# A transformer layer on one core: the causal mask of the row maxima moved from TensorE to VectorE

## The chip, the core and the metric

The kernel runs on one core of a Trainium2 chip, in one launch. The core has TensorE (matrix products into PSUM), VectorE, ScalarE and GpSimd (elementwise work, reductions, masks), and queues that issue DMAs. Each engine runs its own instruction stream in order; they wait for one another through semaphores. The metric is the device time of one execution in microseconds, and the time of the kernel before is the median of three runs.

## The reference, cut to what matters

Four sublayers, each on the layer norm of a residual stream of 16 x 256 tokens with 128 channels: attention a, a mixture of experts, attention b, the same experts again. Both attentions have 16 heads and a causal mask. Attention a, cut (b has no latent space and no rotary tables, and a query and key of 8 channels a head):

```python
q_lat = q @ q2l_w.T + q2l_b                       # 32 latent channels a head; k_lat, v_lat likewise
q_lat = q_lat * cos + _rotate_half(q_lat) * sin   # k_lat likewise
q_for_k = q_lat @ wqk_w.T + wqk_b
att = jnp.einsum('bhql,bhkl->bhqk', q_for_k, k_lat) * L ** (-0.5)
att = jnp.where(causal[None, None], att, -jnp.inf)
att = jax.nn.softmax(att, axis=-1)
y_lat = jnp.einsum('bhqk,bhkl->bhql', att, v_lat)
...
return y @ cproj_w.T + cproj_b
```

## The kernel before, in words

**Stages.** Attention a, experts, attention b, experts run one after the other, each written out once per engine as that engine's instruction stream. An attention handles the 4096 tokens in 8 chunks of 512 (two sequences of 256), and each chunk in 8 units: one sequence and one group of four heads. So there are 64 units an attention.

**A unit.** For each of its four heads, TensorE makes *straight* scores, queries on partitions and keys along the row, in PSUM banks 0 to 3, one bank a head. Only three blocks of 128x128 are made, since the fourth lies above the diagonal: columns 0 to 127 hold the first 128 queries against the first 128 keys, columns 128 to 383 the second 128 queries against all 256 keys. The straight scores serve one purpose: the maximum of every row. VectorE takes it with the sign turned, into M (`row_max` in b, L858 and L859, over four heads at once; `pair_max` in a, L866 and L867, over two heads at once). TensorE turns M (`turn_max`, L1440), and the turned maxima are added to the *turned* scores, keys on partitions, in banks 4 and 5, two heads (a *pair*) at a time. ScalarE takes the exponential of a pair (`exponent`, L1176) into PT, GpSimd sets what lies above the diagonal to zero in PT (`mask`, L548), and TensorE multiplies PT with the values (`weighted`, L1451), one unit later.

**The mask, twice.** For the exponentials GpSimd's zeroes are enough. For the maxima the mask comes from TensorE: `causal` (L1433) opens each bank's accumulation with a matmul of an identity with a block of 0 and -1e30, written to the two diagonal blocks of the bank; the straight scores are added on top.

**How the maxima reach the turned scores.** In a, ScalarE copies the turned maxima (`copy_max`, L1215), and two more matmuls add them (L1499, L1501). In b, VectorE adds them to the query (`join_max`, L933), and the turned scores are made with that sum (L1575, L1579).

**Order.** The order of the work is written out by hand. In a, TensorE's unit is: turn_max, causal of banks 2 and 3, perhaps a projection (`second`), phase 0 (turned scores of heads 0 and 1 of this unit beside straight scores of heads 2 and 3 of the next), another projection, causal of banks 0 and 1, phase 1 (the other heads), a closing step, the value product of the unit before. In b it is: turn_max, causal of banks 2 and 3, a projection (`early`), a wait for join_max, causal of banks 0 and 1, all straight scores of the next unit, turned scores of pair 0, the value product of the unit before, another step (`late`), turned scores of pair 1. On VectorE the maxima stand between the closing work of the projections and the closing steps: the swap of rotary halves (L888, L890) and the low parts of queries (L896) in a; the query's closing (L830), the experts' rows (L1135) and join_max in b; layer norm statistics (L712 to L721) in both. GpSimd does the masks and, in a, the rotary tables' products (L568, L578) and the keys' low parts (L584), in b the keys' sums (L616) and gathers (L649).

**Semaphores around the change.** s_ready (TensorE: straight scores are there) is waited for by the maxima; max_ready (VectorE) by turn_max; mt_ready by copy_max or join_max; exp_done by the masks and by the turned scores that reuse the banks; masked by the value product.

Of the kernel before, what the change touches and what calls it, by code (L numbers as in the profile page):

```python
# [17 lines left out]
P = 128  # L18
# [4 lines left out]
G = 4  # L23
# [287 lines left out]
def program(nc, x, c_attn_w, c_attn_b, q2l_w, q2l_b, kv2l_w, kv2l_b, l2o_w, l2o_b, wqk_w, wqk_b, cproj_w, cproj_b,  # L311
# [7 lines left out]
    with ExitStack() as ctx:  # L319
# [15 lines left out]
        ident_b = sb("ident_b", [P, P], BF16)  # L335
        causal_b = sb("causal_b", [P, P], BF16)
# [35 lines left out]
        with ExitStack() as att:  # L372
# [3 lines left out]
            PT = sb("PT", [P, 2, G, 3 * P], F32, att)  # L376
# [155 lines left out]
        def _(pool):  # L532
# [172 lines left out]
        def _(dve):  # L705
# [73 lines left out]
            for dst, src in ((ident_b, "ident"), (causal_b, "causal"), (before_b, "before"), (sel_r, "sel")):  # L779
                own.did(v.tensor_copy(dst[:, :], con(src)))  # L780
# [73 lines left out]

            def row_max(m, unit, first):

                dve.wait_ge(m["s_ready"], unit + 1)
                v.tensor_reduce(M[:, 0, first::L], PS[:, 0:4, 0:P], AX, ALU.max, negate=True)  # L858
                v.tensor_reduce(M[:, 1, first::L], PS[:, 0:4, P:3 * P], AX, ALU.max, negate=True).then_inc(m["max_ready"], 1)  # L859

            def pair_max(m, unit, pair):
# [3 lines left out]
                banks, cols = slice(2 - 2 * pair, 4 - 2 * pair), slice((2 - 2 * pair) * L, (4 - 2 * pair) * L, L)  # L865
                v.tensor_reduce(M[:, 0, cols], PS[:, banks, 0:P], AX, ALU.max, negate=True)  # L866
                ins = v.tensor_reduce(M[:, 1, cols], PS[:, banks, P:3 * P], AX, ALU.max, negate=True)  # L867
# [282 lines left out]
        def _(act):  # L1150
# [194 lines left out]
        def _(pe):  # L1345
# [83 lines left out]
            def causal(banks):  # L1429

                for j in banks:
                    diagonal = bank[j].rearrange("p (a k) -> p a k", k=P)[:, 0:3:2, :]
                    t_.matmul(diagonal, ident_b[:, :], causal_b[:, :].unsqueeze(1).broadcast_to([P, 2, P]), start=True, stop=False,  # L1433
                              skip_group_check=True)

# [7 lines left out]
            def weighted(m, unit, g, b_, at):  # L1443
# [12 lines left out]
            def attention_a():  # L1456
# [11 lines left out]
                def phase(unit, pair, next_unit):  # L1468
# [12 lines left out]
                    for term, (q, k, kt, qt) in enumerate(((q_h, k_h, k_h, q_h), (q_l, k_h, k_l, q_h), (q_h, k_l, k_h, q_l))):  # L1481
                        if ni is not None:
                            for j, at in straight:
                                t_.matmul(bank[at][:, P:3 * P], q[rows[j], ni % 3, nb, P:S], k[rows[j], ni % 3, nb, :], start=False, stop=False, skip_group_check=True)  # L1484
                        if unit >= 0:
                            for j, at in turned:
                                t_.matmul(bank[at][:, 0:S], kt[rows[j], i3, b_, 0:P], qt[rows[j], i3, b_, :], start=(term == 0), stop=False, skip_group_check=True)
# [5 lines left out]
                        if unit >= 0:  # L1493
                            for j, at in turned:
                                t_.matmul(bank[at][:, S:S + P], kt[rows[j], i3, b_, P:S], qt[rows[j], i3, b_, P:S], start=False, stop=False, skip_group_check=True)
                    if unit >= 0:
                        pe.wait_ge(m["mt_copied"], unit + 1)
                        for j, at in turned:
                            t_.matmul(bank[at][:, 0:S], sel_r[rows[j], :], max_t[rows[j], :, :].rearrange("p b q -> p (b q)"), start=False, stop=False, skip_group_check=True)  # L1499
                        for j, at in turned:  # L1500
                            ins = t_.matmul(bank[at][:, S:S + P], sel_r[rows[j], :], max_t[rows[j], 1, :], start=False, stop=True, skip_group_check=True)  # L1501
# [14 lines left out]
                causal(range(4))  # L1516
# [3 lines left out]
                for unit in range(end):  # L1520
                    turn_max(m, unit)
                    if unit + 1 < end:
                        causal((2, 3))
# [5 lines left out]
                    if unit + 1 < end:  # L1529
                        causal((0, 1))  # L1530
# [12 lines left out]
            def attention_b():  # L1543
# [7 lines left out]
                def scores(unit):  # L1551
# [14 lines left out]
                def turned_scores(unit, pair):  # L1566
# [22 lines left out]
                causal(range(4))  # L1589
# [7 lines left out]
                for unit in range(end):  # L1597
                    turn_max(m, unit)
                    if unit + 1 < end:
# [118 lines left out]
```

## Time and profile before

| what | value |
|---|---|
| median of 3 runs | 1306.4 us (1304.73 to 1308.03) |
| span of the profiled execution | 1331.7 us; the profile gives no other time for that execution |
| instructions | 31337 |
| TensorE busy (matmuls) | 1046.3 us, 79% of the span |
| GpSimd / VectorE / ScalarE busy | 837.9 / 818.4 / 640.7 us |
| mean granted TensorE clock | 0.856 of 2.4 GHz |

How to read it: the profiled execution is one of its own, with its own span; the median is of unprofiled runs. In rows of instructions PE is TensorE, DVE VectorE, ACT ScalarE, POOL GpSimd; PEld is TensorE's loading of weights. An L number is a line of the kernel before. "out<-in" names tiles; the shape is partitions x elements of one instruction. "idle before" is time in which the engine stood still ahead of such instructions, with what ended it. The chain of waits is followed back from the last instruction of a stretch, at each step to what released it; its shares say what set the time. The granted clock is a share of 2.4 GHz, so 0.50 is 1.2 GHz.

### The profile page before, as it was taken

The numbers are of one execution on the slowest core, as the hardware profiler recorded it, in microseconds if no ns is written. First come the engines' busy times: TensorE is split into PE (matmuls) and PEld (weight loads), VectorE is DVE, ScalarE is ACT, GpSimd is POOL, SyncE is SP. The second block draws the span as 40 slices with busy tenths as digits, with TensorE's granted clock in tenths as the row PEclk, the third lists the DMA queues.
The fourth block names the chain that finished last, engine by engine and source line by source line (L and its number), as shares of the span: only waits on it lengthen the run. The fifth ranks groups of instructions, "written<-read, shape, count | busy, mean of one in ns | idle before, by whom it ended". The sixth has DMA issues, their size and how long they took to land.

```text
span 1331.7 us, 31337 instructions
## 1 busy us (share of the span) xinstructions
PE 1046.3 (79%) x11163; PEld 811.0 (61%) x11164; DVE 818.4 (61%) x2025; ACT 640.7 (48%) x1182; POOL 837.9 (63%) x1141
## 2 busy tenths in 40 slices
PE   2699999999999746999925889999998368999300
PEld 1567676677766535999923456666665258999300
DVE  3667877778777375556525667777765573565222
ACT  0266776776766301555513557767765104555100
POOL 0469999999988337555245667777554085553476
PEclk8579999999998756899966789999999558999755
DMA  9000000000000001232300000000000002323222
GB/s 238 1 2 2 2 10 10 2 10 10 2 10 10 9 24 28 66 77 77 58 26 19 20 13 25 24 16 21 10 9 9 32 10 59 80 76 66 57 76 76
DMA packets 56245, 45.69 MB, mean 34 GB/s; under 512 B 13570, under 2 KB 48258, under 8 KB 56130
## 3 DMA queue, kind: packets, MB, share of 16 engines
q0 software_dynamic: 9088, 18.63, 6.3%
q1 hardware_dynamic: 39378, 22.44, 5.9%
q10 hardware_dynamic: 7664, 3.04, 1.0%
q8 instruction: 78, 1.28, 0.4%
q14 instruction: 37, 0.30, 0.1%
HBM read 27.57 MB, written 16.52 MB: 33 GB/s over the span
## 4 chain that ended last, share of the span: by engine, by line
PE 61%; DVE 15%; POOL 8%; ACT 5%; issue 5%; DMA 3%; ACTq 1%; DVEq 1%; another core or an unknown queue 0%; POOLq 0%
PE PS L1667 11%; PE PS L1382 7%; POOL got L649 5%; PE PS L1484 5%; PE PS L1384 5%; PE PS L1383 5%; PE PS L1451 5%; PE PS L1433 3%; PE PS L1440 3%; DVE M L859 2%; PE PS L1464 2%; DMA b_cols<-in_L_ffn_b_dram 2%; PE PS L1422 1%; PE PS L1400 1%; PE PS L1632 1%
## 5 line engine op out<-in xcount | busy, mean ns | idle before, releaser
L548 POOL TENSOR_SCALAR_AFFINE_SELECT PT<-PT 128x256 f32<-128x256 f32 x512 | 218.7, 450 | 109.3 <-ACT PT L1176 107.8
L1176 ACT ACTIVATE PT<-PS 128x768 f32<-128x768 f32 x256 | 206.8, 808 | 116.0 <-PE PS L1579 59.4
L678 POOL DMA_INDIRECT xg<-normed,source x156 | 150.1, 962 | 118.2 <-PE PS L1645 81.7
L649 POOL DMA_INDIRECT got<-expert_rows,slot_of x128 | 122.0, 953 | 79.0 <-DMA expert_rows<-y_rows 46.3
L1308 ACT ACTIVATE hid<-PS,b_cols 128x256 f32<-128x256 f32 x312 | 122.2, 475 | 98.1 <-PE PS L1384 82.3
L1667 PE MATMUL PS<-W,hid 128*128 x1248 | 156.3, 279 | 5.7 <-ACT hid L1308 3.3
L1667 PEld LDWEIGHTS PS<-W,hid 128*128 128x128 f32 x1248 | 149.6, 195 | 6.9 <-issue 6.9
L1451 PE MATMUL PS<-PT,v_aug 128*32 128x256 f32 (+1 forms) x2048 | 115.8, 346 | 2.3 <-POOL PT L548 2.2
L1433 PE MATMUL PS<-causal_b,ident_b 128*128 128x256 bf16 x512 | 103.6, 286 | 10.6 <-DVE q_aug L933 8.3
L1135 DVE SCALAR_TENSOR_TENSOR X<-got,weight,X 128x128 f32<-128x128 f32 x128 | 49.1, 386 | 89.7 <-DMA got<-expert_rows,slot_of 84.0
L866 DVE TENSOR_REDUCE M<-PS 128x2 f32<-128x256 f32 x128 | 54.2, 423 | 73.5 <-PE PS L1490 72.9
L1382 PE MATMUL PS<-xg_hi,w_hi 128*128 128x256 f32 x312 | 96.9, 311 | 1.2 <-issue 1.0
L1383 PE MATMUL PS<-xg_hi,w_lo 128*128 128x256 f32 x312 | 89.8, 288 | 1.8 <-issue 1.8
L568 POOL TENSOR_TENSOR straight<-whole,C 128x512 f32<-128x512 f32 x64 | 83.5, 1305 | 12.2 <-ACT whole L1195 12.2
L1384 PE MATMUL PS<-xg_lo,w_hi 128*128 128x256 f32 x312 | 89.7, 287 | 1.5 <-issue 1.5
L1107 DVE TENSOR_TENSOR y_rows<-PS,b_rows 128x256 f32<-128x256 f32 x78 | 33.2, 425 | 92.9 <-PE PS L1667 80.1
L867 DVE TENSOR_REDUCE M<-PS 128x2 f32<-128x512 f32 x128 | 87.2, 681 | 0.0
L1299 ACT ACTIVATE xg_hi<-PS 128x256 fp32r<-128x256 f32 x78 | 30.0, 385 | 117.0 <-PE PS L1645 117.0
L1161 ACT ACTIVATE xn<-X,shift,rstd 128x128 f32<-128x128 f32 x128 | 55.3, 483 | 57.3 <-POOL shift L541 57.3
L1451 PEld LDWEIGHTS PS<-PT,v_aug 128*32 128x32 f32 x2048 | 55.4, 113 | 41.2 <-issue 10.8
L859 DVE TENSOR_REDUCE M<-PS 128x4 f32<-128x1024 f32 x64 | 77.8, 1216 | 0.0
L1440 PE MATMUL PS<-C,M 128*128 128x128 f32 x256 | 58.3, 311 | 24.6 <-DVE M L859 10.3
(266 smaller groups left out, 3163.9 us busy)
## 6 DMA issues: line engine op xcount, KB each, us to landing
expert_rows<-y_rows SPq DMA_DIRECT2D x78, 128.0 KB
normed<-xn SPq DMA_DIRECT2D x16, 256.0 KB, 2.3
xg<-normed,source POOLq DMA_INDIRECT x156
W<-in_L_ffn_w_dram SPq DMA_DIRECT2D x1, 2048.0 KB, 15.6
got<-expert_rows,slot_of POOLq DMA_INDIRECT x128, 2.6
out_dram<-X SPq DMA_DIRECT2D x8, 256.0 KB
b_rows<-in_L_ffn_b_dram SPq DMA_DIRECT2D x2, 512.0 KB, 3.6
X<-in_L_attn_a_x_dram ACTq DMA_DIRECT2D x2, 256.0 KB, 4.7
```

The lines of the kernel that those rows point to most:

```text
L548: ins = nc.gpsimd.affine_select(out=diagonal, in_=diagonal, pattern=[[0, 2], [1, P]], compare_op=ALU.is_ge, fill=0.0, base=0, channel_mult ...
L649: nc.gpsimd.indirect_dma_start(out=got[:, k, :], out_offset=None, in_=rows_out, in_offset=bass.IndirectOffsetOnAxis(ap=slot_of[:, which * ...
L678: nc.gpsimd.indirect_dma_start(out=xg[:, i % 4, b_, :], out_offset=None, in_=normed, in_offset=bass.IndirectOffsetOnAxis(ap=source[:, k:k ...
L859: v.tensor_reduce(M[:, 1, first::L], PS[:, 0:4, P:3 * P], AX, ALU.max, negate=True).then_inc(m["max_ready"], 1)
L1176: s.activation(PT[:, unit % 2, 2 * pair:2 * pair + 2, :], PS[:, 4:6, 0:3 * P], ACT.Exp).then_inc(m["exp_done"], 1)
L1308: ins = s.activation(hid[:, r % 2, k, :], h_bank[r % 2][k // 2][:, k % 2 * ROWS:(k % 2 + 1) * ROWS], ACT.Gelu, bias=b1_cols[:, bass.ds(e * ...
L1382: t_.matmul(o, w_hi, x_hi, start=start, stop=False, skip_group_check=True)
L1383: t_.matmul(o, w_lo, x_hi, start=False, stop=False, skip_group_check=True)
L1384: return t_.matmul(o, w_hi, x_lo, start=False, stop=True, skip_group_check=True)
L1433: t_.matmul(diagonal, ident_b[:, :], causal_b[:, :].unsqueeze(1).broadcast_to([P, 2, P]), start=True, stop=False, skip_group_check=True)
L1451: ins = t_.matmul(bank[6][j * L:(j + 1) * L, at + kb * P:at + S], v_aug[:, unit // UNITS % 2, 2 * b_ + kb, g * G + j, :], PT[:, unit % 2, ...
L1667: ins = t_.matmul(y_bank[r % 2][:, b_ * P:(b_ + 1) * P], hid[:, r % 2, k, b_ * P:(b_ + 1) * P], W2[:, bass.ds(e * F + k * D, D)], start=(k ...
```

## The change

TensorE no longer writes the mask into the straight scores' banks: `causal` and its two constant tiles go, and the straight scores open their own accumulation. VectorE adds the mask while it takes the maximum, with one fused operation for each head and each half of the queries: it adds the mask to the scores, multiplies by -1, writes that back to the bank, and leaves the minimum in M. The mask tile past_mask is 128x256: zeroes, then the causal block. So that the two diagonal blocks of a head lie side by side in PT, the turned scores of the second 128 keys move to columns 0 to 127 and the others behind them; PT gets an order of blocks, then heads, and one select of GpSimd clears all four diagonal blocks of a pair.

The diff, cut (in a, the turned scores, their added maxima and the value products get the new columns in the same way as shown for b):

```diff
-        causal_b = sb("causal_b", [P, P], BF16)
+        past_mask = sb("past_mask", [P, 2 * P])
...
-            PT = sb("PT", [P, 2, G, 3 * P], F32, att)
+            PT = sb("PT", [P, 2, 2, 3, 2, P], F32, att)
...
             def mask(m, unit, pair):
-                for j in (2 * pair, 2 * pair + 1):
-                    diagonal = PT[:, unit % 2, j, :].rearrange("p (a q) -> p a q", q=P)[:, 0::2, :]
-                    ins = nc.gpsimd.affine_select(out=diagonal, in_=diagonal, pattern=[[0, 2], [1, P]], compare_op=ALU.is_ge, fill=0.0,
-                                                  base=0, channel_multiplier=-1)
-                ins.then_inc(m["masked"], 1)
+                diagonals = PT[:, unit % 2, pair, 0:2, :, :].rearrange("p a h q -> p (a h) q")
+                nc.gpsimd.affine_select(out=diagonals, in_=diagonals, pattern=[[0, 4], [1, P]], compare_op=ALU.is_ge, fill=0.0,
+                                        base=0, channel_multiplier=-1).then_inc(m["masked"], 1)
...
+            own.did(v.memset(past_mask[:, 0:P], 0.0))
...
-            for dst, src in ((ident_b, "ident"), (causal_b, "causal"), (before_b, "before"), (sel_r, "sel")):
+            for dst, src in ((before_b[:, :], "before"), (sel_r[:, :], "sel"), (past_mask[:, P:2 * P], "causal")):
...
+            def head_max(j, column):
+                for q, cols, mask in ((0, slice(0, P), past_mask[:, P:2 * P]), (1, slice(P, 3 * P), past_mask[:, :])):
+                    ins = v.tensor_tensor_reduce(bank[j][:, cols], bank[j][:, cols], mask, -1.0, 3e38, ALU.add, ALU.min, M[:, q, column:column + 1])
+                return ins
...
             def row_max(m, unit, first):
-                v.tensor_reduce(M[:, 0, first::L], PS[:, 0:4, 0:P], AX, ALU.max, negate=True)
-                v.tensor_reduce(M[:, 1, first::L], PS[:, 0:4, P:3 * P], AX, ALU.max, negate=True).then_inc(m["max_ready"], 1)
+                for j in range(G):
+                    ins = head_max(j, j * L + first)
+                ins.then_inc(m["max_ready"], 1)
             def pair_max(m, unit, pair):
-                v.tensor_reduce(M[:, 0, cols], PS[:, banks, 0:P], AX, ALU.max, negate=True)
-                ins = v.tensor_reduce(M[:, 1, cols], PS[:, banks, P:3 * P], AX, ALU.max, negate=True)
+                for j in (2 - 2 * pair, 3 - 2 * pair):
+                    ins = head_max(j, j * L)
...
-                s.activation(PT[:, unit % 2, 2 * pair:2 * pair + 2, :], PS[:, 4:6, 0:3 * P], ACT.Exp).then_inc(m["exp_done"], 1)
+                s.activation(PT[:, unit % 2, pair, :, :, :], PS[:, 4:6, 0:3 * P].rearrange("p h (a q) -> p a h q", q=P), ACT.Exp).then_inc(m["exp_done"], 1)
...
-            def causal(banks):
...
-                                        PT[:, unit % 2, j, kb * S:kb * P + S], start=(unit % G == 0 and kb == 0), stop=(g % 2 == 1 and kb == 1),
+                                        PT[:, unit % 2, j // 2, 1 - kb:3 - 2 * kb, j % 2, :], start=(unit % G == 0 and kb == 0), stop=(g % 2 == 1 and kb == 1),
...
 # attention b: straight scores, turned scores, the two calls of causal
-                        t_.matmul(bank[j][:, 0:P], qs[rows, c % 2, g, b_, 0:P], ks[rows, c % 2, g, b_, 0:P], start=False, stop=False, skip_group_check=True)
+                        t_.matmul(bank[j][:, 0:P], qs[rows, c % 2, g, b_, 0:P], ks[rows, c % 2, g, b_, 0:P], start=True, stop=False, skip_group_check=True)
-                        t_.matmul(bank[4 + k][:, 0:S], ks[rows, c % 2, g, b_, 0:P], q_aug[rows, :, :].rearrange("p b q -> p (b q)"), start=True, stop=False,
+                        t_.matmul(bank[4 + k][:, P:3 * P], ks[rows, c % 2, g, b_, 0:P], q_aug[rows, :, :].rearrange("p b q -> p (b q)"), start=True, stop=False,
-                        ins = t_.matmul(bank[4 + k][:, S:S + P], ks[rows, c % 2, g, b_, P:S], q_aug[rows, 1, :], start=False, stop=True,
+                        ins = t_.matmul(bank[4 + k][:, 0:P], ks[rows, c % 2, g, b_, P:S], q_aug[rows, 1, :], start=False, stop=True,
-                    if unit + 1 < end:
-                        causal((2, 3))
                     if plan.early[unit]:
                         step(plan.early[unit])
                     if unit + 1 < end:
                         pe.wait_ge(m["aug_ready"], unit + 1)
-                        causal((0, 1))
                         scores(unit + 1)
```

## Rows read from the trace of the kernel before

**Rows 1.** The page, whole execution: span, busy share of engines, TensorE's busy tenths in 40 slices.

```profile
span 1331.7 us, 31337 instructions
...
PE 1046.3 (79%) x11163; PEld 811.0 (61%) x11164; DVE 818.4 (61%) x2025; ACT 640.7 (48%) x1182; POOL 837.9 (63%) x1141
...
PE   2699999999999746999925889999998368999300
```

**Rows 2.** Windows, eight units each: length, busy PE PEld DVE ACT POOL, clock, DMA share, GB/s.

```profile
213.00:260.74 47.74, 47.43 (x705) 33.55 (x704) 37.64 (x92) 33.59 (x57) 43.77 (x58) 1.00 0.03 8
849.50:886.64 37.14, 34.67 (x380) 23.08 (x376) 29.18 (x68) 26.52 (x41) 28.81 (x50) 1.00 0.08 23
```

**Rows 3.** Chain of waits by line, attention a, 213 to 260.7 us.

```profile
by line: PE PS L1484 18.8%; PE PS L1451 9.9%; PE PS L1464 9.2%; PE PS L1382 7.6%; PE PS L1433 6.2%; PE PS L1499 5.0%; PE PS L1440 4.4%; PE PS L1384 4.3%; PE PS L1383 4.3%; PE PS L1490 4.3%; DVE M L867 2.5%; PE PS L1422 2.3%; PE PS L1426 2.1
```

**Rows 4.** Chain of waits by line, attention b, 849.5 to 886.6 us.

```profile
by line: DVE M L859 12.2%; PE PS L1382 9.0%; PE PS L1451 8.5%; DVE qs L830 8.1%; DVE M L858 6.7%; ACT minus L1262 6.1%; PE PS L1384 5.6%; PE PS L1383 5.6%; PE PS L1433 5.5%; PE PS L1440 4.5%; PE PS L1575 3.8%; PE PS L1559 3.5%; issue 3.5%; 
```

**Rows 5.** Waits in b, 849.5 to 886.5 us: us in total, times, longest.

```profile
PEld PS L1440 <- DVE M L859: 2.4, 6, 0.8
```

**Rows 6.** Waits in a, 213 to 260.7 us.

```profile
DVE M L866 <- PE PS L1490: 7.0, 10, 1.1
...
PEld PS L1440 <- DVE M L867: 0.5, 1, 0.5
```

**Rows 7.** Timeline of TensorE in b, one unit: start, us, instruction.

```profile
852.05 0.38 PE L1433 MATMUL PS<-causal_b,ident_b 128*128 128x256 bf16 x2
...
853.30 0.39 PE L1433 MATMUL PS<-causal_b,ident_b 128*128 128x256 bf16 x2
```

**Rows 8.** Timeline of VectorE in a.

```profile
219.38 0.88 DVE L822 TENSOR_TENSOR v_aug<-PS,a_v_bias 128x128 f32<-128x128 f32 x4 [1.48 <-PE PS L1384]
...
222.88 0.42 DVE L866 TENSOR_REDUCE M<-PS 128x2 f32<-128x256 f32 x1 [0.20 <-PE PS L1490]
223.22 0.68 DVE L867 TENSOR_REDUCE M<-PS 128x2 f32<-128x512 f32 x1
223.82 0.35 DVE L836 RECIPROCAL inv_sum<-PS 128x32 f32<-128x32 f32 x1
...
230.92 0.38 DVE L718 BATCH_NORM_AGGREGATE mv<-stats 128x2 f32<-128x6 f32 x4
```

**Rows 9.** Timeline of VectorE in b.

```profile
849.90 0.68 DVE L858 TENSOR_REDUCE M<-PS 128x4 f32<-128x512 f32 x1
...
851.63 0.35 DVE L836 RECIPROCAL inv_sum<-PS 128x32 f32<-128x32 f32 x1
```

**Rows 10.** Single lines of VectorE: count, shortest/median/longest ns, first and last start.

```profile
L822 DVE TENSOR_TENSOR v_aug<-PS,b_v_bias x32: 277/280/292, 706.5 to 974.6; 128x128 f32<-128x128 f32 x32
...
L718 DVE BATCH_NORM_AGGREGATE mv<-stats x128: 147/149/183, 19.9 to 1040.6; 128x2 f32<-128x6 f32 x128
```

**Rows 11.** Groups by line: busy us, mean ns of one, idle before and its end.

```profile
L1107 DVE TENSOR_TENSOR y_rows<-PS,b_rows 128x256 f32<-128x256 f32 x78 | 33.2, 425 | 92.9 <-PE PS L1667 80.1
...
L548 POOL TENSOR_SCALAR_AFFINE_SELECT PT<-PT 128x256 f32<-128x256 f32 x512 | 218.7, 450 | 109.3 <-ACT PT L1176 107.8
...
L1215 ACT ACTIVATE max_t<-PS 128x256 fp32r<-128x256 f32 x64 | 24.5, 383 | 45.2 <-PE PS L1440 45.2
...
L1299 ACT ACTIVATE xg_hi<-PS 128x256 fp32r<-128x256 f32 x78 | 30.0, 385 | 117.0 <-PE PS L1645 117.0
```

**Rows 12.** Single lines of VectorE, two SBUF inputs and one.

```profile
L890 DVE TENSOR_TENSOR swapped<-swapped,C x64: 691/786/1775, 48.2 to 429.7; 128x512 f32<-128x512 f32 x64
...
L830 DVE SCALAR_TENSOR_TENSOR qs<-PS,b_bias,minus x32: 740/751/752, 690.7 to 989.8; 128x512 fp32r<-128x512 f32 x32
```

**Rows 13.** Windows of 4 us in b's first chunks.

```profile
744.00:748.00 4.00, 1.28 (x5) 0.62 (x5) 3.58 (x16) 1.69 (x3) 3.25 (x5) 0.76 0.00 1
748.00:752.00 4.00, 4.00 (x33) 2.35 (x31) 2.13 (x3) 0.81 (x1) 2.72 (x5) 0.50 0.15 37
...
804.00:808.00 4.00, 2.75 (x37) 1.91 (x37) 3.23 (x10) 2.94 (x6) 2.01 (x4) 1.00 0.12 31
```

More of the change, by code:

```diff
@@ L778, in _ @@
             dve.wait_ge(rest_loaded, 16 * N_REST)
-            for dst, src in ((ident_b, "ident"), (causal_b, "causal"), (before_b, "before"), (sel_r, "sel")):
-                own.did(v.tensor_copy(dst[:, :], con(src)))
+            for dst, src in ((before_b[:, :], "before"), (sel_r[:, :], "sel"), (past_mask[:, P:2 * P], "causal")):
+                own.did(v.tensor_copy(dst, con(src)))
             dve.wait_ge(pe_prep, 6)
@@ L853, in closing @@
                                     gate_bias[:, :].unsqueeze(1).broadcast_to([P, CT, E]), ALU.add).then_inc(m["freed_dve"], 1)
+            def head_max(j, column):
+                for q, cols, mask in ((0, slice(0, P), past_mask[:, P:2 * P]), (1, slice(P, 3 * P), past_mask[:, :])):
+                    ins = v.tensor_tensor_reduce(bank[j][:, cols], bank[j][:, cols], mask, -1.0, 3e38, ALU.add, ALU.min, M[:, q, column:column + 1])
+                return ins
             def row_max(m, unit, first):
                 dve.wait_ge(m["s_ready"], unit + 1)
-                v.tensor_reduce(M[:, 0, first::L], PS[:, 0:4, 0:P], AX, ALU.max, negate=True)
-                v.tensor_reduce(M[:, 1, first::L], PS[:, 0:4, P:3 * P], AX, ALU.max, negate=True).then_inc(m["max_ready"], 1)
+                for j in range(G):
+                    ins = head_max(j, j * L + first)
+                ins.then_inc(m["max_ready"], 1)
             def pair_max(m, unit, pair):
                 dve.wait_ge(m["s_ready"], 2 * unit + pair + 1)
-                banks, cols = slice(2 - 2 * pair, 4 - 2 * pair), slice((2 - 2 * pair) * L, (4 - 2 * pair) * L, L)
-                v.tensor_reduce(M[:, 0, cols], PS[:, banks, 0:P], AX, ALU.max, negate=True)
-                ins = v.tensor_reduce(M[:, 1, cols], PS[:, banks, P:3 * P], AX, ALU.max, negate=True)
+                for j in (2 - 2 * pair, 3 - 2 * pair):
+                    ins = head_max(j, j * L)
                 if pair == 1:
@@ L1427, in common @@
                 ins.then_inc(m["w_ready"], 1)
-            def causal(banks):
[L1431 to L1434, printed above, removed]
             def turn_max(m, unit):
@@ L1483, in phase @@
                             for j, at in straight:
-                                t_.matmul(bank[at][:, P:3 * P], q[rows[j], ni % 3, nb, P:S], k[rows[j], ni % 3, nb, :], start=False, stop=False, skip_group_check=True)
+                                t_.matmul(bank[at][:, P:3 * P], q[rows[j], ni % 3, nb, P:S], k[rows[j], ni % 3, nb, :], start=(term == 0), stop=False, skip_group_check=True)
                         if unit >= 0:
                             for j, at in turned:
-                                t_.matmul(bank[at][:, 0:S], kt[rows[j], i3, b_, 0:P], qt[rows[j], i3, b_, :], start=(term == 0), stop=False, skip_group_check=True)
+                                t_.matmul(bank[at][:, P:3 * P], kt[rows[j], i3, b_, 0:P], qt[rows[j], i3, b_, :], start=(term == 0), stop=False, skip_group_check=True)
                         if ni is not None:
@@ L1494, in phase @@
                             for j, at in turned:
-                                t_.matmul(bank[at][:, S:S + P], kt[rows[j], i3, b_, P:S], qt[rows[j], i3, b_, P:S], start=False, stop=False, skip_group_check=True)
+                                t_.matmul(bank[at][:, 0:P], kt[rows[j], i3, b_, P:S], qt[rows[j], i3, b_, P:S], start=False, stop=False, skip_group_check=True)
                     if unit >= 0:
@@ L1498, in phase @@
                         for j, at in turned:
-                            t_.matmul(bank[at][:, 0:S], sel_r[rows[j], :], max_t[rows[j], :, :].rearrange("p b q -> p (b q)"), start=False, stop=False, skip_group_check=True)
+                            t_.matmul(bank[at][:, P:3 * P], sel_r[rows[j], :], max_t[rows[j], :, :].rearrange("p b q -> p (b q)"), start=False, stop=False, skip_group_check=True)
                         for j, at in turned:
-                            ins = t_.matmul(bank[at][:, S:S + P], sel_r[rows[j], :], max_t[rows[j], 1, :], start=False, stop=True, skip_group_check=True)
+                            ins = t_.matmul(bank[at][:, 0:P], sel_r[rows[j], :], max_t[rows[j], 1, :], start=False, stop=True, skip_group_check=True)
                         ins.then_inc(m["st_ready"], 1)
@@ L1515, in attention_a @@
                         pe.wait_ge(m["freed_dve"], s.freed)
-                causal(range(4))
                 phase(-1, 0, 0)
@@ L1528, in attention_a @@
                         step(plan.project[unit])
-                    if unit + 1 < end:
-                        causal((0, 1))
                     phase(unit, 1, unit + 1)
@@ L1587, in value_product @@
                     weighted(m, unit, g, b_, g // 2 * S)
-                causal(range(4))
                 for s in plan.prologue:
@@ L1598, in attention_b @@
                     turn_max(m, unit)
-                    if unit + 1 < end:
-                        causal((2, 3))
                     if plan.early[unit]:
@@ L1604, in attention_b @@
                         pe.wait_ge(m["aug_ready"], unit + 1)
-                        causal((0, 1))
                         scores(unit + 1)
```

1 line of the change is left out of this document (removed).

## The prediction

> **What bounds the kernel now.** I read the page first: no engine is busy all the time, and the 40 slices show four stages, two attentions, a in slices 3 to 13 with TensorE at 9 tenths and b in slices 22 to 31 with 8 to 9 after its first, and an expert stage behind each [rows 1]. The change touches only the attentions, so I then took one steady chunk of eight units out of each [rows 2]. In a, eight units take 47.74 us, 5.97 a unit, and TensorE is busy for 47.43 of them; GpSimd with 43.77 (5.47 a unit) and VectorE with 37.64 (4.70 a unit) have little room behind it. In b, eight units take 37.14 us, 4.64 a unit, and no engine fills them: TensorE 34.67, VectorE 29.18, GpSimd 28.81. The granted clock is 1.00 in both, TensorE's 2.4 GHz.
>
> The chain of waits says what each stage goes by. In a the chain is TensorE nearly throughout; the causal matmuls (L1433) are 6.2% of it and the second reduction of the maxima (L867) 2.5% [rows 3]. In b the two reductions of row_max lead: L859 12.2% and L858 6.7%, with the causal matmuls at 5.5% [rows 4]. The waits agree: in b TensorE's turn of the maxima (L1440) waits for L859 in 6 of 8 units, in a in one of 8, while it is VectorE there that waits for scores (L866, 7.0 us a chunk) [rows 5, 6].
>
> **The change part by part.** *Causal matmuls.* 512 go, four a unit. What they are worth is their share of the chain, not their busy time: 6.2% of 47.74 us is 2.96 us, 0.37 a unit in a; 5.5% of 37.14 is 2.04 us, 0.26 a unit in b. In b a pair stands between the turn of the maxima and the next projection, another between that and the next scores [rows 7]. In units where the query's closing on VectorE (L830) comes after the projection, it holds row_max up and the second pair is hidden; so b gets less.
>
> *Row maxima.* Per unit four reductions in a, two in b, become eight fused operations, each 128x128 or 128x256, masks from SBUF, scores from PSUM, written back to PSUM. VectorE overlaps the end of one instruction with the next, so I go by starts. A 128x256 reduction starts 0.34 us before its successor, a 128x512 one 0.60: 0.94 a pair of heads, 1.88 a unit in a [rows 8]. In b it is 849.90 to 851.63, 1.73 a unit [rows 9]. For the new operation the nearest are tensor operations on PSUM with an SBUF operand: four of 128x128 end after 0.88 us, the last lasting 0.28, so 0.20 from start to start [rows 8, 10]; for 128x256, 0.34 as above. A head costs 0.54 us by this.
>
> No row shows what handing over the minimum costs. Below: nothing. Above: a small operation that overlaps nothing, 0.149 us (L718), behind a full 0.280 and 0.425 [rows 10, 11]: 1.00 a head. A slower write to PSUM, which no row shows either (a second pass over the 384 elements, 0.39 at the 0.26 that 256 more elements cost a reduction), ends near the same, 0.93. I take a small operation in a row: four of L718 end after 0.38 us, (0.38 - 0.149) / 3 = 0.077 each [rows 8, 10], since VectorE overlaps neighbours everywhere else. That gives 0.54 + 0.154 = 0.694 a head, 2.78 a unit; the ends are 2.16 and 4.00. On this the Trainium skill (VectorE: DVE Perf Modes, "Two Vector instructions with no wait between them") says that an operation that also writes out its accumulator is two instructions, the main one and an accumulator read; no row before shows one. The same page ("The TRN2 errata") gives 120 cycles plus the elements at 0.96 GHz for a PSUM source, 0.258 and 0.392 us, an estimate of 0.65 a head that would end near 1319 us; the trace has 0.280 for the first from end to end and 0.20 from start to start, and the trace decides.
>
> *VectorE's load.* In a, 4.70 - 1.88 + 2.78 = 5.60 a unit; TensorE's chain there becomes 5.97 - 0.37 = 5.60. Two engines with equal loads that wait for each other twice a unit don't both run without a gap: I let half of the 0.37 go and keep 0.18. The 63 units after the first give -12 us. Low end: VectorE 4.98, all of 0.37 kept, -23 us. High end: 4.70 - 1.88 + 4.00 = 6.82, +0.85 a unit, +54 us.
>
> In b the maxima grow by 2.78 - 1.73 = 1.05 a unit. They are on the chain for 18.9% of 37.14 us, 7.02 of the 13.84 us that eight units spend on them, so in half of the units they set the pace; in the others TensorE comes a little later and eats some of the 1.05. I count 0.8 of it: 0.84 - 0.26 = +0.58 a unit, +37 us over 63. Low end: half of 0.43, less 0.26, -0.04, -3 us. High end: 2.27, less a slack of 0.15 and the 0.26, +1.86, +117 us.
>
> No wait is added, but max_ready comes later. Behind it on TensorE stand the projection, the next scores and the turned scores; copy_max on ScalarE (in a) and join_max on VectorE (in b) wait for the turn. The wait for the join stays ahead of the scores, so nothing runs earlier there.
>
> *GpSimd.* One select of 512 elements a pair of heads replaces two of 256 that average 0.450 us [rows 11]. Bounds: 0.45 to 0.90, so between nothing and 0.9 us a unit saved. No line of GpSimd is among the leading ones of either chain [rows 3, 4], and its 5.47 in a stays under 5.60 at either end: I take zero. If VectorE cost nothing, 5.47 would be the next floor.
>
> *The rest, at nothing.* The exponential reads PSUM in another order; a strided read of 128x256 takes 383 ns and a plain one 385 [rows 11]. ScalarE is busy for 33.59 of 47.74 us, which would hide 0.2 us an instruction (two a unit); beyond that it would surface. The turned scores and value products keep their columns. At the start a memset replaces a copy, beside TensorE's own preparation. Contention of VectorE with GpSimd for SBUF: operations with two SBUF inputs spread from 691 to 1775 ns (L890), one with PSUM and SBUF only from 740 to 752 (L830) [rows 12]; the new one is of the second kind, so nothing.
>
> **The sum.** -12 + 37 = +25 us. The profiled span is 1331.7 us, 25.3 above the median of the runs, 1306.4; the differences are taken over unscaled (1.9% of 25 us is 0.5), so 1306.4 + 25 = 1331 us. With the low ends -26, 1280; with the high ends +171, 1477. What a run of this kernel can tell from no change is about 0.3%, 3.9 us.
>
> **The rivals.** *The minimum comes for nothing (faster).* A head costs 0.54: a keeps 0.37 a unit, b is flat, 1280 us. For it: TensorE is the full chain of a, and every row of b's low end is measured. Against it: the result must leave through something. It decides below 0.61 us a head: there a still gains 0.28 a unit (18 us) and b loses (2.44 - 1.73) x 0.75 - 0.26 = 0.27, 17 us.
>
> *Each hand-over waits until the fused operation has ended (much slower).* Near 0.86 a head (0.280 + 0.425 + 2 x 0.077), VectorE leads in a with 6.26, +0.3 a unit, 19 us; b has (3.44 - 1.73) less 0.15 and 0.26, +1.30, 82 us: 1407 us. For it: a minimum can't leave before the last element is through, and that is what the 0.280 of L822 has over its 0.20. Against: every short operation in rows 8 overlaps its neighbour [rows 8]. From 0.80 a head it is this case.
>
> *The clock (slower).* In b's first chunk TensorE was busy for 1.28 of 4 us from 744 and ran at 0.50, 1.2 GHz, from 748 to 752 [rows 13]. The removed matmuls filled such gaps. TensorE would still be busy for some 4.0 of 5.2 us in b, and at 2.75 of 4, from 804, the clock held 1.00 [rows 13], so I don't expect it; at half clock the 4 us of work would be 8 a unit, (8 - 5.2) x 8 = 22 us for each chunk of b that loses it.
>
> *The change does nothing* would need the gain of a to equal the loss of b, heads of about 0.59 to 0.625.
>
> **How the numbers follow.** Heads of 0.625 to 0.80 (small overlapped hand-over), my forecast: 0.42, with a range of its own from 1311 to 1376 (at 0.80: a +6, b +64). Above 0.80, or with a lost clock: 0.25. About 0.59 to 0.625: 0.10. Below: 0.23. Slower is thus 0.67, same 0.10, faster 0.23. The range runs from 1284 to 1420: it cuts off the very lowest end, 0.05, and heads above 0.88, 0.12.
>
> **What would show it.** No L1433; VectorE rows of 128x128 and 128x256 at 0.28 and 0.42 us and a start-to-start of about 0.28 and 0.42 with a short row between; a chunk of a at about 46 us with VectorE busy for 45 of them, a chunk of b at about 42 us with the row maxima over 30% of its chain and every turn of the maxima waiting for VectorE. The prediction is wrong if a head's two operations start less than 0.61 us apart together, if GpSimd or ScalarE ends a's chain, or if TensorE's clock leaves 1.00 in b's steady chunks.

## The result and the profile after

The changed kernel takes 1369.67 us, median of 4 runs (1358.14 to 1378.8), the one before 1307.22 beside it: a ratio of 1.0431, 95% interval 1.0388 to 1.0473. The prediction said slower, by 25 us; it is 62 between the medians and 56 by the ratio. The ratio and its interval leave out executions far above the fastest of their kernel, here the changed kernel's profiled one at 1378.8, so they can differ from the medians.

The page of the changed kernel, whole execution; PEclk is TensorE's granted clock in tenths of 2.4 GHz:

```profile
span 1377.1 us, 31721 instructions
...
PE 1056.6 (77%) x10651; PEld 812.1 (59%) x10652; DVE 905.0 (66%) x3689; ACT 641.7 (47%) x1182; POOL 801.1 (58%) x885
...
PE   2699999999998557999357788888888647999400
...
PEclk9568999997999757999756788878785557999755
```

TensorE's busy time has grown against [rows 1], by 10 us, although 512 matmuls are gone. So the matmuls that are left have become slower, and the clock row shows where: slices 21 to 32, attention b, stand at 5 to 8 tenths.

Windows of the changed kernel: eight units of a, eight of b, all of a, all of b. Columns as in [rows 2].

```profile
213.00:260.30 47.30, 44.61 (x674) 31.24 (x672) 42.08 (x190) 33.72 (x58) 41.32 (x42) 1.00 0.03 8
862.89:907.05 44.16, 37.05 (x348) 24.12 (x351) 35.67 (x180) 26.49 (x42) 26.50 (x34) 0.84 0.07 19
...
70.04:456.71 386.67, 362.19 (x5198) 254.26 (x5198) 322.49 (x1433) 255.14 (x427) 312.33 (x311) 0.93 0.02 6
712.05:1077.64 365.59, 306.45 (x2623) 196.73 (x2626) 270.70 (x1364) 199.13 (x302) 189.33 (x238) 0.75 0.05 14
```

All of a and all of b in the kernel before:

```profile
712.17:1024.94 312.77, 278.41 (x2867) 181.29 (x2866) 219.38 (x484) 199.46 (x302) 206.74 (x364) 0.93 0.06 17
69.61:447.34 377.73, 370.63 (x5448) 261.50 (x5448) 288.70 (x678) 254.03 (x428) 330.98 (x437) 0.97 0.02 6
```

Of the 45.4 us between the two spans, b brings +52.8 and a +8.9; the rest, which the change doesn't touch, takes back 16.4 (641.2 us in the kernel before, 624.8 in the changed one and 623.9 in select_only below, so it is before's execution that stands out). The steady chunk of a is 0.4 us shorter than in [rows 2]. The +8.9 of a come from two other chunks, which ran at 0.70 and 0.86. So most of the loss is in b: its chunk grew from 37.14 to 44.16 us, and its clock fell from 1.00 to 0.84.

The new operation in a, timeline of VectorE in the changed kernel:

```profile
217.39 0.29 DVE L856 CUSTOM_DVE_ANT_0 PS<-PS,past_mask 128x128 f32<-128x128 f32 x1
217.60 0.14 DVE L856 DVE_READ_ACCUMULATOR2_ANT M<- 128x1 f32 x1
217.60 0.47 DVE L856 CUSTOM_DVE_ANT_0 PS<-PS,past_mask 128x256 f32<-128x256 f32 x1
217.98 0.14 DVE L856 DVE_READ_ACCUMULATOR2_ANT M<- 128x1 f32 x1
217.98 0.33 DVE L856 CUSTOM_DVE_ANT_0 PS<-PS,past_mask 128x128 f32<-128x128 f32 x1
218.23 0.14 DVE L856 DVE_READ_ACCUMULATOR2_ANT M<- 128x1 f32 x1
218.23 0.47 DVE L856 CUSTOM_DVE_ANT_0 PS<-PS,past_mask 128x256 f32<-128x256 f32 x1
218.61 0.14 DVE L856 DVE_READ_ACCUMULATOR2_ANT M<- 128x1 f32 x1
```

Each fused operation is two instructions, as the Trainium skill says (VectorE: DVE Perf Modes, "Two Vector instructions with no wait between them"); here the second starts together with the next fused operation. From start to start, 128x256 takes 0.38 us and 128x128 0.25, but 0.21 for the first, which has no accumulator read beside it: a head is 0.63 us, four heads 2.52.

GpSimd's select, groups by line and form:

```profile
L546 POOL TENSOR_SCALAR_AFFINE_SELECT PT<-PT 128x512 f32<-128x512 f32 x256 | 184.1, 719 | 157.9 <-ACT PT L1180 157.6
```

It takes 719 ns for a pair of heads; two of 450 [rows 11] did before.

The chain of waits of the changed kernel by line, attention a from 213.00 to 260.30 us (in b, from 862.89 to 907.05, the fused operation, L856, leads with 28.3% and 6.6%, against 18.9% for the reductions in [rows 4]):

```profile
by line: PE PS L1481 11.3%; ACT PT L1180 10.2%; DVE PS L856 8.8%; PE PS L1461 8.5%; PE PS L1448 8.3%; ACT q_w L1205 5.9%; PE PS L1437 3.2%; ACT q_h L1207 3.2%; PE PS L1386 3.1%; DVE swapped L892 3.0%; DVE swapped L894 2.9%; PE PS L1496 2.9%
```

Its waits in the same stretch of a (L1481: turned scores, L1437: the turn of the maxima; us in total, times, longest):

```profile
PEld PS L1481 <- ACT PT L1180: 4.2, 8, 0.6
...
PEld PS L1437 <- DVE M L856: 2.6, 6, 1.5
...
PE PS L1437 <- DVE M L856: 1.3, 1, 1.3
```

And in b:

```profile
PEld PS L1437 <- DVE M L856: 6.0, 6, 1.7
...
PE PS L1437 <- DVE M L856: 4.0, 5, 1.5
```

The kernel before in b, beside [rows 5]:

```profile
PE PS L1440 <- DVE M L859: 1.5, 3, 0.7
```

PEld's waits run beside PE's, so each is compared with its own. The weights of the turn wait 6.0 us a chunk of b, where they waited 2.4 [rows 5], and its matmuls 4.0 against 1.5; in a the weights wait 2.6 against 0.5 [rows 6]. In a ScalarE's exponential, L1180, now stands in the chain too: the weights of the turned scores wait 4.2 us a chunk for it. The kernel before, same stretch of a:

```profile
PEld PS L1484 <- ACT PT L1176: 1.7, 8, 0.2
```

### The profile page after: what moved, and what is told of

It reads as the page before. It is cut to its first block, busy times and chain, and to the rows that moved or that the text cites. A ratio compares the mean times of both kernels' runs of the same rounds, so it can differ in the third digit from the quotient of the medians.

```text
span 1377.1 us, 31721 instructions
## 1 busy us (share of the span) xinstructions
PE 1056.6 (77%) x10651; PEld 812.1 (59%) x10652; DVE 905.0 (66%) x3689; ACT 641.7 (47%) x1182; POOL 801.1 (58%) x885
## 4 chain that ended last, share of the span: by engine, by line
PE 54%; DVE 22%; ACT 8%; POOL 6%; issue 4%; DMA 4%; ACTq 1%; DVEq 1%; POOLq 0%
PE PS L1655 10%; DVE PS L856 9%; PE PS L1386 6%; PE PS L1448 5%; PE PS L1388 5%; PE PS L1387 5%; POOL got L646 5%; PE PS L1481 4%; PE PS L1437 3%; PE PS L1461 2%; ACT PT L1180 2%; DVE M L856 2%; DMA b_cols<-in_L_ffn_b_dram 2%; ACT minus L1266 2%; PE PS L1404 2%
## 5 line engine op out<-in xcount | busy, mean ns | idle before, releaser
L856 DVE CUSTOM_DVE_ANT_0 PS<-PS,past_mask 128x128 f32<-128x128 f32 (+1 forms) x1024 | 331.1, 393 | 87.7 <-PE PS L1487 52.8
L546 POOL TENSOR_SCALAR_AFFINE_SELECT PT<-PT 128x512 f32<-128x512 f32 x256 | 184.1, 719 | 157.9 <-ACT PT L1180 157.6
L1180 ACT ACTIVATE PT<-PS 128x768 f32<-128x768 f32 x256 | 206.8, 808 | 125.4 <-PE PS L1571 78.8
L1655 PE MATMUL PS<-W,hid 128*128 x1248 | 152.6, 276 | 1.3 <-ACT hid L1312 1.2
L1655 PEld LDWEIGHTS PS<-W,hid 128*128 128x128 f32 x1248 | 146.4, 192 | 2.1 <-issue 2.1
L856 DVE DVE_READ_ACCUMULATOR2_ANT M<- 128x1 f32 x1024 | 145.7, 142 | 0.0
L1448 PE MATMUL PS<-PT,v_aug 128*32 128x256 f32 (+1 forms) x2048 | 136.6, 395 | 2.2 <-POOL PT L546 2.2
L1437 PE MATMUL PS<-C,M 128*128 128x128 f32 x256 | 64.3, 339 | 53.4 <-DVE M L856 39.0
L1448 PEld LDWEIGHTS PS<-PT,v_aug 128*32 128x32 f32 x2048 | 61.0, 125 | 51.3 <-issue 25.5
L613 POOL TENSOR_TENSOR ks<-whole,minus 128x512 fp32r<-128x512 f32 x32 | 41.0, 1280 | 68.7 <-ACT minus L1266 68.7
L661 POOL TENSOR_SCALAR block_hot<-C,block_f 128x78 fp32r<-128x78 f32 x64 | 46.8, 732 | 46.0 <-DVE scratch L1051 42.5
```

The lines of the kernel that those rows point to most:

```text
L546: nc.gpsimd.affine_select(out=diagonals, in_=diagonals, pattern=[[0, 4], [1, P]], compare_op=ALU.is_ge, fill=0.0, base=0, channel_multipli ...
L856: ins = v.tensor_tensor_reduce(bank[j][:, cols], bank[j][:, cols], mask, -1.0, 3e38, ALU.add, ALU.min, M[:, q, column:column + 1])
L1180: s.activation(PT[:, unit % 2, pair, :, :, :], PS[:, 4:6, 0:3 * P].rearrange("p h (a q) -> p a h q", q=P), ACT.Exp).then_inc(m["exp_done"], 1)
L1437: ins = t_.transpose(bank[q][:, 3 * P:4 * P], M[:, q, :], ident)
L1655: ins = t_.matmul(y_bank[r % 2][:, b_ * P:(b_ + 1) * P], hid[:, r % 2, k, b_ * P:(b_ + 1) * P], W2[:, bass.ds(e * F + k * D, D)], start=(k ...
```

## The experiments

Two theories. *Clock*: what goes beyond the sum is TensorE dropping to 1.2 GHz in b, because the removed matmuls had filled its waits and the waits for the maxima have grown. *Long maxima*: the fused operations alone cost it, and the clock is a side effect that costs nothing.

### One attention at a time: a_only, b_only

The diffs below are excerpts; a minus is the changed kernel.

```diff
 # a_only: in b, causal and the two reductions stay (b_only: the same for a)
-                for j in range(G):
-                    ins = head_max(j, j * L + first)
...
+                v.tensor_reduce(M[:, 0, first::L], PS[:, 0:4, 0:P], AX, ALU.max, negate=True)
+                v.tensor_reduce(M[:, 1, first::L], PS[:, 0:4, P:3 * P], AX, ALU.max, negate=True).then_inc(m["max_ready"], 1)
```

> The change in attention a alone; b keeps its reductions and its causal matmuls (with the new column order and the one select in both). Theory 1 (the loss is TensorE's clock in b: longer waits for the maxima let it fall to 0.50): a gains 0.44 us a chunk where the clock holds and loses a few us where it falls at its start, so 1303 to 1312, b's stage as long as before and its clock near 1.00. Theory 2 (the loss is the longer row maxima by themselves, the same in kind in both attentions): a heads' price of 0.63 leaves a at -10 to 0, so 1297 to 1307. Neither expects more than 1315; above it the loss sits in a and both fall.

> The change in attention b alone; a keeps its reductions and its causal matmuls. Theory 1: most of the loss, 1345 to 1365, with a granted clock of 0.7 to 0.85 over b's stage. Theory 2: the same time, 1345 to 1365, but then the clock is a by-product, and the maxima's 0.79 us a unit must account for 45 us, so that units at a clock of 1.00 are as long as the others.

a_only: 1314.96 us (10 runs), ratio 1.0024 [0.9993, 1.0054]. b_only: 1369.1 (4 runs), 1.0435 [1.0381, 1.0488]. Windows of a_only: a steady chunk of a, all of a, all of b:

```profile
215.74:263.01 47.27, 44.57 (x673) 31.27 (x673) 42.05 (x188) 33.69 (x59) 41.26 (x41) 1.00 0.03 8
70.46:442.31 371.85, 345.83 (x5198) 242.29 (x5198) 322.62 (x1433) 254.75 (x428) 313.00 (x312) 0.98 0.02 6
701.55:1008.56 307.01, 273.25 (x2867) 177.94 (x2866) 220.28 (x484) 199.57 (x302) 190.35 (x238) 0.96 0.06 17
```

And of b_only, all of b:

```profile
699.54:1070.24 370.70, 312.61 (x2623) 201.00 (x2626) 270.85 (x1364) 199.22 (x303) 189.34 (x238) 0.73 0.05 14
```

b alone brings the whole loss. a is worth -0.47 us a steady chunk, some 4 us in 64 units, and nothing that the runs can tell. Neither total was forecast by either theory: a_only lies above 1303 to 1312 and 1297 to 1307, b_only above 1345 to 1365. Nor is a always free of the clock: it stands at 0.98 in a_only, but in gap_fill1 and gap_fill (below), whose a is that of the changed kernel, it took 385.1 us at 0.93 and 377.3 at 0.96.

### The select and the layout alone: select_only

All of causal and the reductions stay; only PT's order, the turned scores' columns and the one select are new.

> The new order of blocks in PSUM and PT and the one select of GpSimd alone; the causal matmuls and the reductions are those of before. Both theories and the prediction: nothing, 1304 to 1312. GpSimd's select takes 719 ns for 512 elements against 2 x 450, and GpSimd leads no chain.

1305.09 us (10 runs), 0.9968 [0.994, 0.9996]: at the edge of what can be told. Its steady chunk of b is the 37.14 us of [rows 2], and its a and b are the measure for the stages in what follows, as its profiled execution (1307.59) lies near the medians:

```profile
793.75:830.89 37.14, 34.76 (x380) 23.08 (x381) 29.24 (x68) 26.57 (x41) 26.67 (x34) 1.00 0.08 23
69.86:442.97 373.11, 366.23 (x5448) 258.94 (x5448) 291.50 (x678) 253.91 (x428) 307.90 (x311) 0.99 0.02 6
697.85:1006.31 308.46, 277.01 (x2871) 180.52 (x2874) 220.12 (x484) 199.68 (x302) 189.97 (x238) 0.94 0.06 17
```

### The long maxima without the removal: both_masks

```diff
 # the changed kernel; causal is called at all its places again, and the straight
 # scores still open their own accumulation (start=True), as in the change
+                    if unit + 1 < end:
+                        causal((2, 3))
```

> The changed kernel with the causal matmuls put back where they stood, as filler: the first straight scores open the accumulation after them and overwrite what they wrote. VectorE does the fused maxima as in the change. Theory 1: they fill TensorE's waits, b's clock comes back to 0.95 or more, and the time falls below the changed kernel, 1335 to 1355, although TensorE has more work. Theory 2: 0.26 us a unit on the chain of b and up to 0.37 in a come back, so it is slower than the changed kernel, 1375 to 1400.

1367.69 us (4 runs), 1.0438 [1.0392, 1.0485]: the expected gain of the clock theory (1335 to 1355) did not come, and the loss that the other expected (1375 to 1400) didn't either. b took 362.7 us at 0.88, where the changed kernel has 0.75. Two chunks of it:

```profile
808.19:850.68 42.49, 34.91 (x380) 23.07 (x382) 34.88 (x180) 26.73 (x42) 27.04 (x34) 1.00 0.08 22
850.68:896.41 45.73, 39.20 (x380) 25.64 (x382) 35.03 (x180) 27.10 (x42) 26.32 (x34) 0.89 0.07 18
```

This prices the fused maxima alone at full clock: 42.49 against 37.14, +0.67 us a unit. It also shows that the longer waits by themselves lose clock in some chunks, with every matmul in its place. The causal matmuls stand behind the turn, on the path, and probably cost in time what they gave back in clock: at 1.00 the chunk is 1.52 us longer than that of gap_fill (below), which has matmuls in the wait instead. The total doesn't decide between the theories. The two chunks say more: the same 380 matmuls, in the same places, take 3.24 us longer at 0.89.

### The removal without the long maxima: no_mask

```diff
 # the changed kernel, but the reductions of before instead of head_max: no mask of the maxima at all
-                for j in range(G):
-                    ins = head_max(j, j * L + first)
...
+                v.tensor_reduce(M[:, 0, first::L], PS[:, 0:4, 0:P], AX, ALU.max, negate=True)
+                v.tensor_reduce(M[:, 1, first::L], PS[:, 0:4, P:3 * P], AX, ALU.max, negate=True).then_inc(m["max_ready"], 1)
```

A row's maximum is thus taken over the scores above the diagonal too. The softmax is the same whatever is subtracted from a row, and GpSimd's zeroes still mask the exponentials.

> The changed kernel with the plain reductions of before and no causal mask in the row maxima at all: the maximum is taken over the 128x128 and 128x256 blocks as they are, an upper bound of the masked one, which cancels in the softmax; GpSimd's zeroes still mask the exponentials. It is the removal from TensorE alone, without VectorE's price. Both theories: the prediction's terms of the removal, 0.37 and 0.26 us a unit, 40 us, so 1267 to 1275. Theory 1 adds that the clock may fall in b more often than before, as the matmuls filled gaps, which would leave 1275 to 1300; theory 2 excludes that.

1309.09 us (10 runs, 1294.56 to 1325.78), 0.9957 [0.9919, 0.9995]: above all that was expected, even the 1275 to 1300 of the clock theory. A kernel that only leaves work out hardly gains. Windows: a steady chunk of a, all of b, a chunk of b:

```profile
209.37:255.50 46.13, 44.30 (x673) 31.24 (x672) 39.03 (x93) 33.60 (x59) 40.82 (x42) 1.00 0.03 8
687.99:1019.95 331.96, 291.13 (x2619) 187.85 (x2618) 220.59 (x484) 198.60 (x302) 190.65 (x238) 0.79 0.06 15
830.78:876.12 45.34, 43.15 (x348) 28.48 (x352) 30.25 (x68) 26.50 (x42) 25.82 (x34) 0.68 0.06 17
```

a gains 1.6 us a chunk. b takes 332 us where select_only takes 308, with less work on TensorE and the same on VectorE; its clock is 0.79. The profiled execution took 1320.81 us, 11.7 above the median, but the granted clock of the whole kernel was lower in every run: 0.813 to 0.849 in these ten, 0.857 to 0.877 in the nineteen of the kernel before beside them. In the chunk at 0.68, TensorE is busy for 43.15 of 45.34 us, so there its slow matmuls, and not its waits, set the time. This is the clock theory without its rival: no long maxima are here.

### Useless matmuls in the waits: gap_fill, gap_fill1, no_mask_gap, no_mask_gap1

```diff
 # b, TensorE, at the end of a unit, ahead of the next turn of the maxima; bank 6, zero weights: adds nothing to it
                     turned_scores(unit, 1)
+                    if unit % G:
+                        for _ in range(3):
+                            t_.matmul(bank[6].rearrange("p (a q) -> p a q", q=P), zero_b[:, :], before_b[:, :].unsqueeze(1).broadcast_to([P, 4, P]),
+                                      start=False, stop=False, skip_group_check=True)
```

gap_fill is the changed kernel with this, no_mask_gap is no_mask with this; the names with a 1 have one matmul instead of three.

> The changed kernel, and in b, in three units of four, three more matmuls of 128x512 with zero weights just ahead of the turn of the maxima, where TensorE waits for VectorE some 1 us a unit; they add zero to the value products' bank, so the result is the same. At full clock they take about 0.64 us, inside the wait. Theory 1 (the lost clock in b is most of the loss): b's clock rises from 0.75 to above 0.9, its chunks go from 44 to 47 us to 40 to 42, and the time falls to 1325 to 1345. Theory 2 (the longer maxima do it by themselves): the work in the wait is hidden or is in the way, 1362 to 1380.

> The kernel without any mask in the maxima (plain reductions), with the same three matmuls in b. There the removal cost b its clock (0.79) and gained 4 us in all. Theory 1: the clock comes back to 0.95 or more, b's chunks go from 37 to 45 us to 34 to 36, and the time falls to 1265 to 1285. Theory 2: no change but for the matmuls themselves, 1305 to 1330.

> The changed kernel with one useless 128x512 matmul, instead of three, ahead of the turn of the maxima in three of four units of b. Clock theory: one fills a third as much of TensorE's wait, so the clock of b lies between that of the changed kernel (0.64 to 0.84 a chunk) and 1.00; chunks of b of 41 to 44 us, a total between 1345 and 1365 us. If three were too much and cost time on the path, it is the fastest of the three, 1335 to 1345. Theory of longer row maxima alone: nothing changes against the changed kernel, 1358 to 1372.

> No causal mask of the maxima on any engine (plain reductions over unmasked blocks), with one useless 128x512 matmul in three of four units of b. The causal matmuls that b lost were 4 x 256 columns a unit, so one of 512 in three of four units gives back 384 of 1024. Clock theory: between no_mask (1309, chunks of b at 0.68 to 0.91) and the run with three (1294, chunks at 1.00 and 37.3 us), or, where one is enough for 1.00, chunks below 37 us and a total of 1280 to 1292. Other theory, that the three matmuls helped by their place and not by the clock: 1292 to 1296 whatever the clock.

| kernel | median us (4 runs each) | ratio | b's chunk at granted clock |
|---|---|---|---|
| gap_fill | 1345.58 | 1.0288 [1.0219, 1.0357] | 40.97 at 1.00 |
| gap_fill1 | 1372.2 | 1.0468 [1.0417, 1.0519] | 42.96 at 0.92, 45.56 at 0.81 |
| no_mask_gap | 1293.9 | 0.9871 [0.9815, 0.9928] | 37.32 at 1.00 |
| no_mask_gap1 | 1291.84 | 0.9858 [0.9797, 0.9919] | 36.17 at 1.00 |

Windows of gap_fill, a chunk of b and all of b:

```profile
808.06:849.03 40.97, 35.33 (x366) 22.11 (x369) 34.42 (x180) 26.41 (x41) 26.61 (x34) 1.00 0.08 21
...
704.77:1046.95 342.18, 286.47 (x2764) 177.23 (x2767) 267.51 (x1364) 198.39 (x303) 189.82 (x238) 0.92 0.06 15
```

Of no_mask_gap1, the same:

```profile
817.42:853.59 36.17, 32.51 (x354) 21.36 (x357) 30.51 (x68) 26.17 (x42) 26.60 (x34) 1.00 0.09 23
...
685.05:987.54 302.49, 260.50 (x2669) 167.91 (x2668) 225.69 (x484) 197.37 (x302) 189.53 (x238) 0.93 0.06 17
```

Of gap_fill1, two chunks of b:

```profile
815.46:858.42 42.96, 36.09 (x354) 22.98 (x356) 34.76 (x180) 26.48 (x41) 26.41 (x34) 0.92 0.08 20
858.42:903.98 45.56, 39.66 (x354) 25.35 (x357) 35.65 (x180) 26.38 (x41) 27.37 (x34) 0.81 0.07 20
```

Added work makes both kernels faster: from 1.0431 to 1.0288 of the kernel before in the changed one (b: 365.6 to 342.2 us), with intervals well apart; from 0.9957 to 0.9871 and 0.9858 in no_mask (b: 332.0 to 302.5 with one), where the intervals just touch. Nothing else was edited, and where the time fell, the clock of nearly all steady chunks had risen to 1.00. So the long-maxima theory is out as the sole cause. The totals were not all forecast: gap_fill ends at the upper edge of its 1325 to 1345, no_mask_gap between the 1265 to 1285 of the clock theory and the 1305 to 1330 of the other. The dose is not the same in both: one matmul is enough where the maxima are short, and does too little where they are long: gap_fill1's b stays at 0.80 in all, and its median missed the expected 1345 to 1365. Its chunks still stand in one order with the others: 45.56 at 0.81, 44.16 at 0.84 (changed kernel), 42.96 at 0.92, 40.97 at 1.00. With three in no_mask the chunk is 1.15 us longer than with one; there the waits are probably too short to hide them.

A rival is that the useless matmuls help by their place and not by the clock. For no_mask_gap1 it expected 1292 to 1296, which 1291.84 can't exclude. The two chunks of gap_fill1 speak against it: the same 354 matmuls in the same places take 42.96 us at 0.92 and 45.56 at 0.81, as in both_masks.

The Trainium skill describes a case of this kind (TensorE: Matmul & The Clock Gate, "A second HAM failure mode: psum-queue depth-cycling"): in another kernel, short idle stretches between groups of matmuls came often enough to make the clock go back and forth between its two levels. The changed kernel's chunk of 44.16 us agrees, with no wait for the maxima longer than 1.7 us.

### a without any mask of the maxima: a_no_mask

In a as no_mask, in b as before, with the new layout and the one select.

> No mask in a's maxima (plain reductions, no causal matmuls), while b keeps its causal matmuls and plain reductions. Theory 1: a keeps its clock at 1.00 and its gain of 1.6 us a chunk, b is as before: 1290 to 1298. Theory 2: the same for a; it has no price for b: 1290 to 1298. If it comes out at 1305 or more, the removal in a lengthens something after a, and both fall.

1295.13 us (4 runs), 0.9866 [0.9814, 0.9919]. A steady chunk of a, and then TensorE's wait for ScalarE in it:

```profile
205.81:251.96 46.15, 44.30 (x673) 31.24 (x673) 38.98 (x92) 33.58 (x58) 40.76 (x42) 1.00 0.03 8
```

```profile
PEld PS L1490 <- ACT PT L1182: 4.2, 8, 0.6
```

TensorE is busy 3.13 us a chunk less than in [rows 2], but the chunk is only 1.59 shorter, 0.20 a unit. The weights' wait for the exponential has grown by 2.5 us, from 1.7 to 4.2: the turned scores need banks 4 and 5 back from ScalarE, and the causal matmuls had filled part of that time.

## Why the prediction was right and wrong

Right: slower, and from b; the time lies inside the range. The last of its signs of being wrong came true: TensorE's clock left 1.00 in b's steady chunks.

**The step that failed is the clock.** It was a rival, dismissed with "at 2.75 of 4, from 804, the clock held 1.00 [rows 13], so I don't expect it", and the sum has nothing for it. In these rows, busy time in a window doesn't tell whether the clock holds. Windows of 4 us of the changed kernel in b:

```profile
862.89:866.89 4.00, 2.49 (x27) 1.36 (x26) 3.87 (x19) 2.60 (x4) 2.80 (x5) 0.89 0.06 16
866.89:870.89 4.00, 4.00 (x31) 2.31 (x31) 2.30 (x13) 2.06 (x3) 1.44 (x2) 0.50 0.07 16
...
886.89:890.89 4.00, 2.49 (x31) 1.66 (x33) 3.01 (x19) 2.06 (x4) 2.42 (x4) 1.00 0.01 1
890.89:894.89 4.00, 3.65 (x41) 2.38 (x33) 3.88 (x19) 2.95 (x6) 2.62 (x4) 1.00 0.07 18
```

And of gap_fill:

```profile
849.03:853.03 4.00, 2.25 (x27) 1.26 (x27) 3.97 (x20) 2.60 (x4) 2.56 (x5) 1.00 0.07 20
853.03:857.03 4.00, 3.90 (x42) 2.32 (x42) 3.09 (x19) 2.50 (x4) 2.13 (x3) 1.00 0.06 16
```

With 2.49 busy microseconds of 4 the clock falls once (0.89, then 0.50) and holds 1.00 once; with 2.25 it holds. A single window that kept its clock was no evidence for a stage of 64 units. The price was too simple as well: 22 us for each chunk that loses the clock supposed all or nothing. It comes and goes inside a chunk: against gap_fill's, five of the eight chunks of b pay 3.2 to 6.5 us; in sum 365.6 - 342.2 = 23 us, with b's mean clock at 0.75 in place of gap_fill's 0.92, where the forecast had nothing.

**The head.** 0.694 us chosen, 0.63 measured. The reason was right and its size too large: by the starts (0.25 with an accumulator read beside it, 0.21 without; 0.38 where the sum had 0.34) the small operation costs some 0.04 us, an estimate, and not 0.077. The estimate of 0.65 from the formula in the Trainium skill (VectorE: DVE Perf Modes, "The TRN2 errata") was nearer: it gives 0.258 and 0.392 us, and the starts are 0.25 and 0.38 apart. That is in part chance, since the formula has no hand-over in it.

**The sum in b at full clock.** Predicted +0.58 a unit; gap_fill has (40.97 - 37.14) / 8 = +0.48. Its parts: the removal -0.12 (no_mask_gap1, (36.17 - 37.14) / 8, its useless matmul included) instead of -0.26, the maxima +0.60 (40.97 against 36.17) instead of +0.84. The split hangs on the dose: against no_mask_gap, with three useless matmuls like gap_fill, it is +0.02 and +0.46. The factor 0.8 was fair: 2.52 - 1.73 = 0.79, of which 0.46 to 0.67 arrive (0.67 in both_masks).

**The sum in a.** Predicted -0.18 a unit, measured -0.06 (47.74 to 47.27). The step "what they are worth is their share of the chain", 0.37, was too large: 0.20 arrives, since the wait for the exponential takes the rest. Then the maxima cost 0.14 (46.15 to 47.27), near the 0.18 let go. VectorE did not become the bound: it is busy for 42.1 of 47.3 us, not 45.

Together at full clock: 63 x 0.48 - 63 x 0.06 = +26 us, beside the predicted +25. That agreement is partly luck: the head was too dear, and both removals were too generous. With the 23 us of lost clock in b it is +49, of 56 by the ratio. In the profiled execution b takes 57 us more than select_only's (365.6 - 308.5): 30 by the sum at full clock, 23 of lost clock, and 4 that are left (gap_fill's second and last chunk ran at 0.89 and 0.80). Its a takes 13.6 more (386.7 - 373.1), where the steady chunks gain: lost clock again, in the two chunks at 0.70 and 0.86. What that costs in the median, no run shows.

**What was put at nothing.** The select, the exponential (a median of 810 ns before and after), the layout: select_only says so.

**Open:** which feature of a stretch decides whether the clock holds, and why a loses it in some executions. Only the amount of useless work in one place was varied, not its place or kind.

## What to carry to other kernels

Before taking work from an engine whose clock follows its activity, look at what that work filled: a matmul of 0.39 us in a wait may be what keeps the others at full speed, as in no_mask_gap1, and the granted clock of the stage is then the first thing to compare. A share of the chain is an upper bound of what a removal gives: name the wait next in line (here ScalarE's exponential, 1.7 us becoming 4.2) and subtract it. And ask whether the work is needed at all: the maxima need no mask as long as no score above the diagonal is so large that the exponentials of its row vanish. The versions that leave it out and keep b's clock, in a alone (a_no_mask, 1295.13) or in both (no_mask_gap, 1293.9, and no_mask_gap1, 1291.84), beat the kernel before by 1.3 to 1.4%; their intervals overlap, so the runs don't rank them.

## What was not expected of the hardware

- A kernel with less work ran hardly faster for it: without the four causal matmuls, b took 332.0 us at a mean clock of 0.79; with one useless matmul of 390 ns in three units of four, 302.5 at 0.93.
- Useless matmuls with zero weights were enough to keep the clock: they brought nearly all of b's steady chunks to 1.00.
- The read of an accumulator, 142 ns in the mean, runs under the next fused operation, at a price of some 0.04 us by the starts, an estimate.
- One select of 512 elements takes 719 ns, 1.6 times one of 256 (450 ns) [rows 11].
